# W1 and seven broadcast rows loaded from GpSimd's queue in place of SP's, in the prologue of a cross-attention layer

## The reference

```
q = heads(x @ Wq + bq);  k = heads(ctx @ Wk + bk);  v = heads(ctx @ Wv + bv)
scores = q @ k.T / sqrt(16);  scores = where(j < i, scores, -1e30)
attn = softmax(scores);  attn[query 0] = 0
h = layer_norm(x + (attn @ v) @ Wo + bo) * ln1_g + ln1_b
out = layer_norm(h + relu(h @ W1 + b1) @ W2 + b2) * ln2_g + ln2_b
```

## Time and profile before

| | |
|---|---|
| time, median of 3 runs | 1664.28 us (1663.89 to 1666.03) |
| the profiled execution's own time | 1661.53 us |
| its span, first to last instruction | 1659.6 us |
| mean granted TensorE clock | 0.986 of full |
| busy: PE, ACT, DVE, POOL | 1616.8, 1547.8, 1436.3, 1381.1 us |
| moved by DMA | 208.99 MB, mean 126 GB/s |

### The profile page before, as it was taken

One profiled execution on the slowest core, in us unless ns is written; L12 is line 12 of the kernel. 1 busy time (PEld: TensorE's weight loads), 2 busy tenths in 40 slices (PEclk: granted clock), 3 DMA queues, 4 the chain that ended last, 5 costly groups with the idle time before them and its releaser, 6 DMA issues.

```text
span 1659.6 us, 54093 instructions
## 1 busy us (share of the span) xinstructions
PE 1616.8 (97%) x16700; PEld 1590.2 (96%) x16700; DVE 1436.3 (87%) x6746; ACT 1547.8 (93%) x5905; POOL 1381.1 (83%) x1352
## 2 busy tenths in 40 slices
PE   4799999999999999999999999999999999999998
PEld 3699999999999999999999999999999999999997
DVE  3788898898898898898898898898898898898885
ACT  3899999999999999999999999999999999999993
POOL 2378888888888888888888888888888888888896
PEclk7799999999999999999999999999999999999999
DMA  8856665656656656656665666755666656665630
GB/s 153 173 121 119 133 136 117 134 131 120 134 135 117 135 132 119 135 132 119 134 136 116 135 132 118 136 133 116 135 134 117 136 133 118 136 135 117 122 76 27
DMA packets 307087, 208.99 MB, mean 126 GB/s; under 512 B 164336, under 2 KB 281968, under 8 KB 306800
## 3 DMA queue, kind: packets, MB, share of 16 engines
q1 hardware_dynamic: 304960, 204.47, 60.5%
q10 hardware_dynamic: 1840, 1.05, 0.3%
HBM read 104.73 MB, written 50.33 MB: 93 GB/s over the span
## 4 chain that ended last, share of the span: by engine, by line
PE 95%; DVE 2%; ACT 1%; SPq 1%; DMA 1%; issue 0%; POOL 0%; DVEq 0%; ACTq 0%; POOLq 0%
PE ps_dense L393 32%; PE ps_dense L404 32%; PE ps_probsT L500 14%; PE ps_scores L490 7%; PE ps_att L518 7%; PE ps_dense L375 2%; ACT probs L595 0%; DVE ps_scores L804 0%; DMA q_stack<-qT 0%; DMA probs<-in_L_xattn_Wk_dram 0%; SPq L253 0%; PE ps_att L417 0%; SPq L247 0%; SPq L269 0%; SPq L290 0%
## 5 line engine op out<-in xcount | busy, mean ns | idle before, releaser
L595 ACT ACTIVATE probs<-ps_scores,negmax 128x128 f32<-128x128 f32 x2048 | 744.1, 413 | 8.5 <-DVE negmax L804 5.2
L1059 POOL TENSOR_TENSOR probs<-probs,recip 128x512 f32<-128x512 f32 x512 | 533.1, 1042 | 134.7 <-DVE recip L787 134.5
L804 DVE CUSTOM_DVE_ANT_0 ps_scores<-ps_scores,mask 128x128 f32<-128x128 f32 x2048 | 527.0, 318 | 69.9 <-PE ps_scores L490 67.7
L595 ACT ACTIVATION_READ_ACCUMULATOR probs<-ps_scores,negmax 128x1 f32 x2048 | 517.3, 253 | 0.0
L404 PE MATMUL ps_dense<-w,hT 128*128 128x256 f32 x3048 | 417.9, 286 | 0.9 <-DVE u L929 0.9
L393 PE MATMUL ps_dense<-zT,w 128*128 128x256 f32 x3072 | 416.9, 285 | 0.9 <-DVE h_f L888 0.5
L1067 POOL TENSOR_TENSOR hT<-h_f,hT 128x512 fp32r<-128x512 f32 x252 | 322.8, 1294 | 90.4 <-DVE h_f L888 90.4
L393 PEld LDWEIGHTS ps_dense<-zT,w 128*128 128x128 f32 x3072 | 381.8, 189 | 1.5 <-issue 0.9
L404 PEld LDWEIGHTS ps_dense<-w,hT 128*128 128x128 f32 x3048 | 377.5, 188 | 1.2 <-DVE u L929 1.1
L612 ACT ACTIVATE probsT<-ps_probsT 128x508 f32<-128x508 f32 x512 | 319.4, 624 | 37.4 <-PE ps_probsT L500 37.4
L500 PE MATMUL ps_probsT<-ident,probs 128*128 128x128 f32 x2048 | 313.1, 275 | 0.0
(11 more groups left out here) (96 smaller groups left out, 2345.2 us busy)
## 6 DMA issues: line engine op xcount, KB each, us to landing
k_stack<-k_spill SPq DMA_DIRECT2D x384, 128.0 KB, 4.5
q_stack<-qT SPq DMA_DIRECT2D x762, 64.0 KB, 2.0
k_spill<-kT SPq DMA_DIRECT2D x128, 256.0 KB, 2.2
c_tok<-in_ctx_dram SPq DMA_DIRECT2D x256, 64.0 KB, 5.0
x_res<-in_x_dram SPq DMA_DIRECT2D x64, 256.0 KB, 3.0
x_tok<-in_x_dram SPq DMA_DIRECT2D x252, 64.0 KB, 2.4
out_dram<-o_tok SPq DMA_DIRECT2D x63, 256.0 KB, 2.7
probsT<-in_L_xattn_W_dram SPq DMA_DIRECT2D x1, 1024.0 KB, 10.7
```

Source lines behind the costliest of these rows:

```text
L595: last = nc.scalar.activation(probs[:, m % 4, i, :], ps_scores[m % 2][:, i, :], ACT.Exp, bias=negmax[:, m % 4, i:i + 1], scale=-1.0, accum ...
L804: last = nc.vector.tensor_tensor_reduce(ps_scores[m % 2][:, i, :], ps_scores[m % 2][:, i, :], mask[:], -1.0, -MASKED, ALU.add, ALU.min, ac ...
L1059: nc.gpsimd.tensor_tensor(probs[:, m % 4], probs[:, m % 4], recip[:, m % 4, :].unsqueeze(2).broadcast_to([P, 4, S]), ALU.mult)\
```

## The change

The seven rows and W1 are no longer issued by SP between Wo and `stack_q(1, 0)`. POOL issues them after its zeroing of `v_sb`, W1 first and then the seven rows, on its own DMA queue. The semaphores and the destinations are the same, and nothing else is moved.

```diff
@@ SP @@
             load_weight(2)
             load_weight(3)
-            for dram, tile in ROWS:
-                sp.dma_start(tile, dram.rearrange("(a n) -> a n", a=1).broadcast_to([P, D])).then_inc(s_wr, 16)
-            load_weight(4)
             for it in ITERATIONS:
                 iteration(it)
@@ POOL @@
             for tile in v_sb:
                 nc.gpsimd.memset(tile[:], 0.0).then_inc(s_vzero, 1)
+            by_chunk = WEIGHTS[4][0].rearrange("(c p) n -> p c n", p=P)
+            for raw, c, n in RAW[4]:
+                nc.gpsimd.dma_start(raw, by_chunk[:, c:c + n, :]).then_inc(s_w[4], 16)
+            for dram, tile in ROWS:
+                nc.gpsimd.dma_start(tile, dram.rearrange("(a n) -> a n", a=1).broadcast_to([P, D])).then_inc(s_wr, 16)
```

## The result

The changed kernel takes 1668.95 us (median of 20 runs, 1665.44 to 1673.3) against 1663.63 us for the kernel before (20 runs, 1661.49 to 1666.03): **5.3 us more**, a ratio of 1.0034 with the 95% interval [1.0026, 1.0041] (the ratios here are of the means, the times are medians). The prediction said 1669.3 us, or 5.0 us more. The profiled execution took 1666.07 us, near the low end of its own spread, with a span of 1664.2 us, 4.6 us above that of the kernel before.

A forecast was written before the change was run, and what follows sets the result against it. The prediction took the prologue to wait for q's DMA landing at 30.46, ahead of a full PE stretch. Its terms 0 + 0 + 5.0 + 0 on the median 1664.28 gave 1669.3 us, range 1663.0 to 1674.0.

The forecast's parts named there:

- Only the prologue can move: From 100 to 1600 us PE has no idle time; a prologue longer by d us makes the kernel d us longer.
- the landing at 30.46: Last stacking DMA of group 0's q, issued at 25.73; everything behind it is computing and shifts with it.
- Point 1: SP loses eight issues, about 3.8 us; scores of group 1 start by PE's own order behind `fold_offset`, so gain 0.
- the relief of SP: SP's stacking of group 1's q can begin 2.4 us sooner; counted as 0, at most 2.4 us without `fold_offset`.
- POOL's issues are hidden: Eight issues from 20.77, about 1 us each, fit into POOL's 14.95 us before its next work; cost 0.
- Contention, 5.0 us: Loads beside SP's queue delay q's landing: W1 3.0 us plus five of seven rows at 0.4 us each.
- The low end of the range: No delay of the landing, less the spread of the runs: 1664.28 - 1.3 = 1663.0 us.
- the rival in which it gave something back: PE gets the full clock for the prologue's products, 3.3 to 4.4 us back, about 1660.5 us; chance 0.07.
- The readers are hidden: W1, wanted at 52.67, and the rows, wanted at 53.56, land well before; cost 0.

The follow-up runs named there:

- run 3: Changed kernel, with POOL waiting until the twelve stacking DMAs of group 0 have landed before it issues the eight loads; 1661.81 us, ratio 0.9994 to before.
- run 4: Changed kernel, with the eight loads issued at about the same time by ACT instead of POOL; 1669.33 us, ratio 1.0035 to before.
- run 6: Kernel before, with SP issuing q's stacking of group 0 ahead of the load of x of group 2; 1663.89 us, ratio 1.0000.
- run 7: Changed kernel, with POOL holding the eight loads until group 0's stacking landed and SP stacking q ahead of x of group 2; 1660.67 us, ratio 0.9979.
- runs 9 and 10: Kernel before, W1 and rows issued late on SP behind the spill of group 1's k; 9 with q stacked ahead of x(2), 1666.91 us; 10 without, 1668.20 us.

## Why the prediction was right

*Only the prologue can move.* Shown: 1541.0 us from the attention product of group 2 to the end in every profile.

*The hinge is the landing at 30.46.* Shown by run 3, where it goes back and the median with it, and by run 4, where landing and profiled time move together (8.0 and 7.9 us). It needs an addition that the prediction had only half: a second gate 26 us later, the landing of group 1's k stack. Point 1 said that the scores of group 1 came by PE's order and not by a landing; true, but by a margin of 0.2 us that no row I quoted gave. I called the relief of SP worth at most 2.4 us were `fold_offset` gone. It shows sooner than that: once the landing comes 2.1 us sooner, the lack of relief costs PE 3.22 us (run 6), and having it turns -0.1 into -3.3 us (run 7).

*POOL's issues are hidden.* Right, at 4.7 us in place of the 8 that I took. In the changed kernel VectorE is almost idle beside them (1.08 us of the 8 from 22 to 30). In run 3 POOL issues from 31.6 to 36.2, with VectorE busy for 4.22 of the 4.80 us from 31.5 to 36.3, and a row's issue still takes 0.54 us.

The Trainium skill ("SBUF — State Buffer", sections "SBUF: two separate sides" and "A bandwidth-pool intuition that's wrong (but worth ruling out)") says that GpSimd can't write a DMA's descriptors while VectorE runs an operation in one of its two-port modes, such as a float32 copy within SBUF, and that one whole DMA then took some 3.1 us. No run here shows this or speaks against it: none of VectorE's instructions beside the issues of run 3 is such a copy, and 0.54 us is the length of an issue, not of a DMA.

*Contention, 5.0 us.* The mechanism was right; that the sum of 5.0 came so near the 5.3 is in part luck, since its parts were off. At the landing it is 3.9 us (4.3 in the second profile). W1 was taken at 3.0 and alone costs 3.2 at the landing and 2.1 in the median; the rows were taken at 2.0 and alone cost 4.3 and 3.3. Alone the two make 7.5 us at the landing, together 3.9, so a sum by loads isn't how the delay builds up. I had priced the rows by their bytes at the best rate, and took two of them to come too late. All seven were issued by 26.7.

Nor is it sure that SP's relief, which I put at 0, is 0: run 3 is 1.7 us faster by its median, within noise. The low end of the range took 1.3 us for the spread of the runs, which no row gives; the kernel before spreads by 4.5 us over its 20 runs.

The changed kernel's remaining 0.7 us in the span above the landing's 3.9 (4.6) are partly PE's: the product of v takes 1.96 us in place of 1.57, at a granted clock of 0.74 (54.0 to 56.6 us) where it had been 0.99 (50.5 to 52.2). So the clock took a little here; the rival in which it gave something back is not seen. That it can weigh more than this is shown by experiment 3.

The Trainium skill ("DMA: Bandwidth & Descriptors", section "Queues, rings and completion order") says that each DMA engine goes round its queues by packets. The trace agrees with it, without singling it out from other ways of sharing: SP's queue moved 188 GB/s while its last stacking DMA was under way before, and 79 GB/s in the changed kernel, with POOL's beside it. DMAs that SP had issued up to 26 us are put off by loads that POOL or ACT issue at 21 to 27. But runs 9 and 10 show that one queue does no better when the big loads simply stand ahead on it.

*The readers are hidden.* Right: W1 lands at 32.1 (22.05 + 10.0), the last row at 37 (26.17 + 10.8), 25 and 20 us before they are wanted.

## What to carry to other kernels

A free slot on another engine's queue is not a free slot on the DMA engines. Before moving a load, look for the DMA that the chain waits for and how far its time to landing is above that of a quiet stretch (6.3 against 2.1 us here): while it is in flight, nothing large should be sent, from any queue. And where a gain is costed at nothing because PE is busy at that point, read by how much the data were early; two gates with 0.2 us between them gave nothing clear of noise one at a time and 3.3 us together. And compare a landing only with its own execution's time: a clock that differs between executions can hide or feign 2 us.

## What the runs showed of the hardware

- The same eight loads delay a DMA in flight more from ACT's queue (11.70 us to landing) than from POOL's (8.39 and 8.74). The medians hardly differ (5.9 and 5.3 us above before), since both profiles of the changed kernel are among its quick executions; between the profiled executions the difference is there (7.9 against 4.5 and 5.2 us). ACT began the loads 1 us sooner (21.08 against 22.05); whether that is enough to make up the 4 us at the landing was not tested.
- Bytes are a poor price for a load's harm to others: alone, the broadcast rows, 1 KB read again for each of 128 partitions, cost 4.7 us of landing per MB, W1 3.0. These are single profiles, and the rows alone cost no less than the rows and W1 together.
- Issuing slows down too, by a rule that isn't known: four issues of Wv took 1.86 us before and 1.92 and 1.86 with W1 or the rows alone on POOL's queue, but 3.82 and 4.88 in the changed kernel, 3.68 with the loads on ACT's queue, and 6.25 with W1 twice. How full the engines are doesn't tell it: over those issues the DMA share was 1.27 before and 1.05 in the changed kernel, and with W1 alone 355 GB/s were moved beside issues of 1.92 us.
- The granted clock of the same 50 matmuls at the same place of the program was 1.00 in some executions and 0.73 in others, worth nearly 2 us (experiment 3).
